# A post-norm attention gate and a top-3 mixture of 12 experts on one core: how the normed rows are split into two f16 parts and transposed, and in which half-turn their transposes, logits and maxima stand

## The reference, cut to what matters

```
o   = sum_k exp(causal scores of the roped q and k)            # one number a row
x1  = layernorm(x + relu(o*fc1_w + fc1_b) @ fc2_w.T + fc2_b)
xa  = x1 @ P_w.T;  C1, C2, C3 = softmax of the 3 largest of 12 logits xa @ U_i.T, else 0
h   = gelu(sum_e C1[:, e] * (x1 @ W1[e].T))
y   = sum_e C2[:, e] * (h @ W2[e].T) + C3 @ b2
out = layernorm(x1 + y)
```

## Time and profile before

| | |
|---|---|
| median of 3 runs | 322.95 us (322.84 to 324.55) |
| profiled execution, its own time | 323.53 us |
| its span, first to last instruction | 321.8 us |
| granted TensorE clock, mean | 0.981 |
| TensorE busy | 282.4 us (88%) |
| VectorE busy | 250.2 us (78%) |
| ScalarE busy | 155.8 us (48%) |
| GpSimd busy | 115.0 us (36%) |
| turns 1 to 5 begin at (C3 transpose) | 139.39, 164.97, 190.55, 216.13, 241.71 us |
| turn 6 and turn 7 begin at | 267.28, 289.77 us |

### The profile page before, as it was taken

One profiled execution on the slowest core, in us unless ns is written; L12 is line 12 of the kernel. 1 busy time (PEld: TensorE's weight loads), 2 busy tenths in 40 slices (PEclk: granted clock), 3 DMA queues, 4 the chain that ended last, 5 costly groups with the idle time before them and its releaser, 6 DMA issues.

```text
span 321.8 us, 6235 instructions
## 1 busy us (share of the span) xinstructions
PE 282.4 (88%) x1976; PEld 191.8 (60%) x1978; DVE 250.2 (78%) x744; ACT 155.8 (48%) x327; POOL 115.0 (36%) x264
## 2 busy tenths in 40 slices
PE   0999999979784989999999999999999997989981
PEld 0444455444333668677677667677678576667770
DVE  0169789999976579689789879888978977887672
ACT  1138747657561381435635634633733753724331
POOL 1000028999999102142332331522333324132221
PEclk9999999999985999999999999999999999999998
DMA  8999999900000000000010001000100010011011
GB/s 232 415 404 229 200 151 211 144 3 0 0 1 0 3 2 0 18 18 18 18 33 17 18 18 29 22 18 18 34 20 16 18 34 19 18 33 26 26 35 37
DMA packets 19235, 20.58 MB, mean 64 GB/s; under 512 B 1600, under 2 KB 18432, under 8 KB 18688
## 3 DMA queue, kind: packets, MB, share of 16 engines
q1 hardware_dynamic: 18480, 19.22, 24.8%
q10 hardware_dynamic: 720, 0.93, 1.0%
HBM read 15.94 MB, written 4.19 MB: 63 GB/s over the span
## 4 chain that ended last, share of the span: by engine, by line
DVE 25%; PE 21%; issue 6%; ACT 5%; POOL 3%; DVEq 0%; POOLq 0%
PE bank L832 17%; DVE early L1202 11%; DVE st L1239 3%; DVE stats L1038 2%; DVE top L1059 2%; ACT x L548 2%; DVE early L1244 2%; PE bank L784 2%; ACT early L657 1%; POOL rstd L391 1%; PE bank L741 1%; DVE mv L1240 1%; ACT x1T L555 1%; ACT early L604 1%; DVE esum L1104 1%
## 5 line engine op out<-in xcount | busy, mean ns | idle before, releaser
L832 PE MATMUL bank<-W,early 128*128 (+1 forms) x630 | 75.5, 273 | 4.4 <-DVE early L1244 2.3
L832 PE MATMUL bank<-W,x1T 128*128 (+1 forms) x630 | 76.9, 277 | 0.5 <-DVE early L1202 0.3
L832 PEld LDWEIGHTS bank<-W,x1T 128*128 128x128 f16 x630 | 60.3, 99 | 19.8 <-DVE early L1202 9.5
L688 PE MATMUL bank<-early,wqk 128*128 128x512 f32 x128 | 64.3, 634 | 8.5 <-DMA gatew<-in_gate 8.5
L1202 DVE SCALAR_TENSOR_TENSOR early<-bank,Csel,early 128x256 f32<-128x256 f32 x124 | 59.3, 479 | 15.0 <-PE bank L832 10.5
L832 PEld LDWEIGHTS bank<-W,early 128*128 128x128 f16 x630 | 60.1, 98 | 14.8 <-DVE early L1244 3.3
L457 POOL TENSOR_SCALAR ve<-mv 128x1 f32<-128x1 f32 x32 | 7.3, 230 | 117.2 <-DVE mv L1240 117.2
L688 PEld LDWEIGHTS bank<-early,wqk 128*128 128x128 f32 x128 | 23.5, 201 | 30.1 <-issue 20.9
L604 ACT ACTIVATE early<-early 128x256 f32<-128x256 f32 x32 | 13.3, 417 | 48.0 <-DVE early L1202 47.9
L499 ACT ACTIVATE qk<-bank 128x512 bf16<-128x512 f32 x32 | 19.0, 594 | 35.6 <-PE bank L688 35.4
L599 ACT ACTIVATE early<-bank,Csel 128x256 f32<-128x256 f32 x31 | 14.6, 472 | 31.0 <-PE bank L832 30.7
(11 more groups left out here) (107 smaller groups left out, 422.3 us busy)
## 6 DMA issues: line engine op xcount, KB each, us to landing
early<-in_xT SPq DMA_DIRECT2D x16, 256.0 KB, 9.8
xs<-in_x SPq DMA_DIRECT2D x32, 128.0 KB, 7.3
out<-early SPq DMA_DIRECT2D x32, 128.0 KB
W<-in_w1T SPq DMA_DIRECT2D x1, 2048.0 KB, 12.0
W<-in_w2T SPq DMA_DIRECT2D x1, 2048.0 KB, 12.3
W<-in_w1T SPq DMA_DIRECT2D x1, 1024.0 KB, 7.6
W<-in_w2T SPq DMA_DIRECT2D x1, 1024.0 KB, 13.8
wqk<-in_wqkT ACTq DMA_DIRECT2D x1, 512.0 KB, 3.8
```

The lines of the kernel that those rows point to most:

```text
L688: mm = pe.matmul(bank[PROJ[n % 2]][:, :], wqk[:, k, g, :], xTb[:, c % 4, k, :, :].rearrange("p s n -> p (s n)"), start=(k == 0), stop=(k = ...
L832: mm = pe.matmul(where[:, 0:DIM], lhs(hx, c), w, start=(k == 0), stop=(k == 5))
```

## The change

For groups 2 to 7 (`ROWWISE = 2`) x1 is split before it is transposed: behind each half of `normed` ScalarE writes the high part of two tiles in row layout into a new tensor xh (128x512, f32 to f16), and GpSimd the low part (x1 minus high part, 128x512). TensorE then transposes eight 128x128 f16 pieces for each half, into the same bank read as f16, and ScalarE copies all 1024 columns of it to x1T in one instruction (`x1T_copy`). VectorE's `x1_low` is gone for these groups. Groups 0 and 1 go the old way. The positions in the turn also change, for all groups of the main stage:

| step | before | after |
|---|---|---|
| TensorE x1_transpose(g, 0), (g, 1) | (2,1), (3,1) | (3,0), next turn's (0,0) |
| TensorE route_logits | (0,1) | (1,0) |
| VectorE route_max | (0,1) | (1,0) |
| VectorE route_strike, two halves | (1,0), (2,0) | both (1,1), behind norm_stats |
| ScalarE exp_route | (1,0) | (2,0), ahead of normed(.., 0) |
| ScalarE bank to x1T, half 0, half 1 | (3,0), (0,0) | (3,1), (0,1) |

```
+        identh = sb("identh", [P, P], F16)
+        xh = sb("xh", [P, 2, 2, 2, DIM], F16)
 (GpSimd)
+            def x1_low(g, h):
+                pool.wait_ge(xhi_done, 2 * (g - ROWWISE) + h + 1)
+                pool.tensor_tensor(xh[:, h, :, 1, :], x1[:, g % 3, 2 * h:2 * h + 2, :], xh[:, h, :, 0, :], ALU.subtract)\
+                    .then_inc(xlo_done, 1)
             def aux(k, s, pos):
-                if (s, pos) == (2, 1) and group(k + 1):
-                    chosen_exps(k + 1)
+                if (s, pos) == (2, 0) and group(k + 2):
+                    x1_low(k + 2, 0)
+                if (s, pos) == (2, 1):
+                    if group(k + 2):
+                        x1_low(k + 2, 1)
+                    if group(k + 1):
+                        chosen_exps(k + 1)
 (ScalarE, end of normed)
+                if g >= ROWWISE:
+                    act.wait_ge(x1_done, 2 * g + h + 1)
+                    if g > ROWWISE:
+                        act.wait_ge(x1T_done, 2 * (g - 1) + h + 1)
+                    act.activation(xh[:, h, :, 0, :], x1[:, g % 3, 2 * h:2 * h + 2, :], ACT.Copy).then_inc(xhi_done, 1)
+            def x1T_copy(g, h):
+                act.wait_ge(x1T_done, 2 * g + h + 1)
+                t = GT * g + 2 * h
+                act.activation(x1T[:, t:t + 2, :, :, :].rearrange("p t l c n -> p (t l c n)"),
+                               bank[XPOSE][:, :].bitcast(F16), ACT.Copy).then_inc(x1lo_done, 1)
             def aux(k, s, pos):
-                if (s, pos) == (1, 0) and group(k + 1):
-                    exp_route(k + 1)
-                if (s, pos) == (2, 0) and group(k + 2):
-                    normed(k + 2, 0)
+                if (s, pos) == (0, 1) and k > 0 and group(k + 1):
+                    x1T_copy(k + 1, 1)
+                if (s, pos) == (2, 0):
+                    if group(k + 1):
+                        exp_route(k + 1)
+                    if group(k + 2):
+                        normed(k + 2, 0)
...
-                if (s, pos) == (3, 0) and group(k + 2):
-                    x1_high(k + 2, 0)
+                if (s, pos) == (3, 1) and group(k + 2):
+                    x1T_copy(k + 2, 0)
 (TensorE, x1_transpose)
+                if g >= ROWWISE:
+                    pe.wait_ge(identh_done, 1)
+                    pe.wait_ge(xlo_done, 2 * (g - ROWWISE) + h + 1)
+                    spread = bank[XPOSE][:, :].bitcast(F16)
+                    for t in range(2):
+                        for l in range(2):
+                            for c in range(NC):
+                                n = 2 * NC * t + NC * l + c
+                                tr = pe.transpose(spread[:, n * P:(n + 1) * P], xh[:, h, t, l, c * P:(c + 1) * P],
+                                                  identh[:, :])
```

More of the change, by code:

```diff
@@ L166, in build @@
         RING, HT = 4, 4
+        ROWWISE = 2
         Z = GT * NR * NE
@@ L202, in build @@
         x1lo_done = sem("x1lo_done")
+        identh_done = sem("identh_done")
+        xhi_done = sem("xhi_done")
+        xlo_done = sem("xlo_done")
         z_done = sem("z_done")
@@ L577, in aux @@
                 if (s, pos) == (0, 0):
-                    if group(k + 1):
-                        x1_high(k + 1, 1)
+                    if k == 0:
+                        x1_high(1, 1)
                     if group(k):
                         C3T_copy(k)
-                if (s, pos) == (1, 0) and group(k + 1):
-                    exp_route(k + 1)
-                if (s, pos) == (2, 0) and group(k + 2):
-                    normed(k + 2, 0)
+                if (s, pos) == (0, 1) and k > 0 and group(k + 1):
[5 more added lines that the diff above has]
+                        normed(k + 2, 0)
                 if (s, pos) == (2, 1) and group(k + 2):
                     normed(k + 2, 1)
-                if (s, pos) == (3, 0) and group(k + 2):
-                    x1_high(k + 2, 0)
+                if (s, pos) == (3, 1) and group(k + 2):
+                    x1T_copy(k + 2, 0)
             def begin(t):
@@ L606, in _ @@
             act.wait_ge(ld_const, 16 * 6)
+            act.activation(identh[:, :], identf[:, :], ACT.Copy).then_inc(identh_done, 1)
             for c in range(NCH):
@@ L738, in x1_transpose @@
                 wait(pe, x1lo_done, 2 * g + h)
+                if g >= ROWWISE:
[8 more added lines that the diff above has]
+                                                  identh[:, :])
+                    tr.then_inc(x1T_done, 1)
+                    return
                 for t in range(2):
@@ L800, in aux @@
             def aux(k, s, pos):
[L801 to L807, removed]
+                if (s, pos) == (0, 0):
+                    if k > 0 and group(k + 1):
+                        x1_transpose(k + 1, 1)
+                    if group(k):
+                        C3_transpose(k)
+                if (s, pos) == (0, 1) and group(k + 2):
+                    fc(k + 2, 1)
+                if (s, pos) == (1, 0) and group(k + 1):
+                    route_logits(k + 1)
                 if (s, pos) == (1, 1) and group(k):
                     bias(k, 0)
-                if (s, pos) == (2, 1):
-                    if group(k):
-                        bias(k, 1)
+                if (s, pos) == (2, 1) and group(k):
+                    bias(k, 1)
+                if (s, pos) == (3, 0):
+                    if group(k + 1):
+                        route_count(k + 1)
                     if group(k + 2):
                         x1_transpose(k + 2, 0)
[L815 to L821, removed]
+                if (s, pos) == (3, 1) and group(k + 3):
+                    fc(k + 3, 0)
             held_ids = {}
@@ L1140, in aux @@
                         fc_add(k + 2, 0)
[L1141 to L1144, removed]
+                    if k == 0:
+                        x1_low(1, 1)
                 if (s, pos) == (1, 0):
@@ L1148, in aux @@
                     if group(k + 1):
-                        route_strike(k + 1, 0)
[L1150 to L1155, removed]
+                        route_max(k + 1)
+                if (s, pos) == (1, 1):
+                    if group(k + 2):
+                        norm_stats(k + 2)
+                    if group(k + 1):
+                        route_strike(k + 1, 0)
                         route_strike(k + 1, 1)
+                if (s, pos) == (2, 0) and group(k):
+                    bias_add(k, 0)
                 if (s, pos) == (2, 1) and group(k + 1):
                     route_mask(k + 1)
[L1159 to L1163, removed]
+                if (s, pos) == (3, 0) and group(k):
+                    bias_add(k, 1)
                 if (s, pos) == (3, 1) and group(k + 1):
```

## The result

| | before | after |
|---|---|---|
| median | 323.13 us (4 runs) | 328.93 us (328.08 to 329.11, 4 runs) |
| ratio | | 1.0165, interval 1.013 to 1.020 |
| profiled execution, span | 323.53, 321.8 us | 329.11, 327.3 us |
| C3 transposes, turns 0 to 7 begin | 101.03, 139.39, 164.97, 190.55, 216.13, 241.71, 267.28, 289.77 | 101.96, 139.53, 166.33, 193.16, 220.00, 246.84, 273.68, 294.98 |

The account below looks back on a forecast made before the run. TensorE (24.19 us busy of a 25.58 us turn) and VectorE (21.95) were taken to bound it, handing work to each other. Turn 0 -1.9, turns 1 to 5 +6.4, turn 6 -0.9: +3.6, 326.6 us, range 321.3 to 330.3.

Parts of the forecast that it names:

- The walk of a full turn: Step-by-step sum of engine queues for turns 1 to 5: 26.87 us against 25.58, +1.29 each, +6.4 for five.
- the second step: Full turn, VectorE overfilled by route_max put in front of norm_stats: transposes at 14.88 against 14.21 before, +0.67 us.
- the third: Full turn, ScalarE's queue with exp and two table loads: gelu to gelu 7.93 us, +1.42 against before.
- the fourth: Full turn, last step: 4.06 us against 4.86, -0.80, as the second x1 transpose and its wait left it.
- the two named losses: Full turns: +0.67 us from VectorE's overfilled second step and +1.42 from ScalarE's queue in the third step.
- TensorE alone would be there at 13.95: Second step: when TensorE by itself would reach the transposes, against 14.88 us by VectorE's path.
- the reserve of 0.27: Third step: TensorE's second mixture ends at 22.54, 0.27 us ahead of the transposes that wait for gelu at 22.81.
- The term of turn 0: Turn 0, with 12 experts in one mixture: turn 1 would begin 1.9 us earlier than at 139.39.
- the adds of the long mixture start 0.8 earlier: Part of the turn 0 gain: VectorE's adds for the 12-expert mixture start 0.8 us earlier.
- The wait of 1.22 us: Turn 0: VectorE's wait for ScalarE's `begin`, which stood behind the table load, was to go.
- Turn 6: Turn with routing but no norm work: forecast 21.57 us instead of 22.49, -0.9.
- The weighed rules: Two skill statements: a 1380 ns drain per table switch, which the trace contradicted, and GpSimd contending with VectorE for SBUF.

Follow-up runs that it names:

- e2_stats_early: Changed kernel with fc_add(k+2, 1) and norm_stats on VectorE moved from (1,0) and (1,1) to (0,1): 322.29 us, ratio 0.994.
- e1_exp_back: Changed kernel with exp_route on ScalarE put back from (2,0) to (1,0): 320.70 us, ratio 0.990.
- e8_mask_early: Changed kernel with route_mask on VectorE at (2,0), ahead of the third step's adds, instead of (2,1): 328.12 us, ratio 1.015.
- e5_positions_alone: Changed kernel with the old split (f32 transposes, x1_low on VectorE) for all groups, new positions kept: 324.01 us, ratio 1.001.
- e7_best: Changed kernel with exp_route at (1,0), route_mask at (2,0), and fc_add and norm_stats at (0,1) except in turn 0: 317.45 us, ratio 0.980.
- e4_split_alone: Changed kernel with every step back at the positions of the kernel before, exp_route at (1,0), row-wise split kept: 334.09 us, ratio 1.032.
- e6_low_twice: Changed kernel with each x1_low on GpSimd done twice, one more subtraction for each half of a group: 332.75 us, ratio 1.026.

## Why the prediction was right

**The walk of a full turn held.** The full turns lose where the prediction said, by +0.7 in the second step, +1.4 in the third, -0.8 in the fourth. Turn 26.87 predicted, 26.84 measured; the second step's transposes at 14.88 behind the C3 transpose, measured 14.92 (208.08 less 193.16); the third step 7.93, measured 7.87; the fourth 4.06, measured 4.04 (215.96 to 220.00). e2_stats_early and e1_exp_back each removed one of the two named losses and left the wait of the other.

**Waits that the walk had otherwise.** It had TensorE wait some 0.9 us for gelu in the second step; it waited 1.19, and for the add ahead of it. "TensorE alone would be there at 13.95" is one pair of transposes too late: the pitches named there sum to 13.58. VectorE's path was last all the same, so this cost the sum nothing. In the third step the walk had no term for the mask. The mask ended behind x1_low (213.28 against 213.04), so TensorE's second mixture ended at 22.80 in place of 22.54 and the reserve of 0.27 was used up: in the trace it ends just where gelu allows the next transposes. That this wait did not set the turn is shown by e8_mask_early.

**Prices.** The xh copy was 0.629 us for 0.63, the subtraction 1.157 for 1.21, eight f16 transposes 0.44 for 0.44, x1T_copy 1.016 for "some 1.0 to 1.2". The 0.63 was a choice between rows of 0.46 and 0.72; that it came out to the digit is luck, and its ends would have moved the turn by 0.2 or 0.3 us.

```profile
L573 ACT ACTIVATE xh<-x x12: 629/629/631, 125.8 to 266.9; 128x512 f16<-128x512 f32 x12
L405 POOL TENSOR_TENSOR xh<-x,xh x12: 1154/1157/1160, 126.5 to 268.0; 128x512 f16<-128x512 f32 x12
```

**What was off by size.** The term of turn 0: "turn 1 begins 1.9 us earlier than at 139.39"; it began 0.14 later. Of the 2 us, 0.93 came ahead of turn 0. Another 0.4 went in its first 13 us, to matmuls at a slower pace. These had a mean clock of 0.86 before and 0.81 here. The rest is the term "the adds of the long mixture start 0.8 earlier": counted from TensorE's transposes of o at the end of that stretch (113.43 before, 114.76 here), they start 9.14 us behind instead of 9.24, 0.1 earlier. The wait of 1.22 us did go, and the two adds that had it start 0.9 us earlier by that measure. But 0.8 of this was lost on VectorE before the long adds: 0.36 from these adds to the low part of hT (with a wait of 0.17 for ScalarE's high part), 0.27 for two strikes that had stood ahead of the wait, and 0.14 at bias_add. What follows the adds came as forecast, 1.09 us shorter for 1.1. Turn 6 was 0.3 us shorter than walked (21.30 for 21.57).

The 0.93 us have this beginning, in the changed kernel:

```profile
8.48 6.74 PE L721 MATMUL bank<-early,wqk 128*128 128x512 f32 x8 [8.48 <-DMA gatew<-in_gate]
15.15 0.63 PE L904 MATMUL bank<-uTs,pws 64*128 64x36 f32 x4
```

From start to start that is 6.67 us; before, the same eight matmuls take 5.64. They run at a pitch of 0.85 us until the clock rises and of 0.43 after, and it rose two to three matmuls later. In the ten experiments, whose beginning is the same as here, the next group starts anywhere from 13.7 to 15.0 us after the span's start (14.17 in the kernel before), and turn 0 at 100.6 to 101.8 (101.03 before, 101.96 here). So nearly all of it is the scatter of one execution and not the change. The profile's +5.5 us holds it; the four executions scatter by 1.7 us in the kernel before and by 1.0 us here.

**The weighed rules.** A table load costs its 1.28 us and the next instruction follows (208.54 to 209.84): the trace again disagrees with the drain that the Trainium skill, "ScalarE: Activation LUTs", section What ACT_TABLE_LOAD costs, adds; with it, by the page's figure and as an estimate, 7.87 would have been 10.6. The other rule showed at a place I had not priced. The mask's first instruction has two SBUF inputs and took 0.55 us beside GpSimd's x1_low in turns 1 to 5, and 0.25 in turns 0 and 6, where GpSimd worked on a 128x1 tile. It took 0.25 in all turns of the kernel before, of e5_positions_alone (same position, no x1_low on GpSimd) and of e7_best (another position). x1_low itself took 1.16 in every instance, beside the mask or not. The trace agrees with the Trainium skill, "GPSIMD Engine Reference", section 8 (Key points), by which VectorE's instructions with two SBUF inputs contend with GpSimd. The timelines of the changed kernel show x1_low, the mask's instruction and, beside the second x1_low, the adds, which read PSUM and stayed as they were (1.00 for the two):

```profile
211.88 1.16 POOL L405 TENSOR_TENSOR xh<-x,xh 128x512 f16<-128x512 f32 x1 [3.86 <-ACT xh L573]
212.60 0.55 DVE L1130 TENSOR_TENSOR mask<-zs,top 128x96 bf16<-128x96 f32 x1
...
214.20 1.00 DVE L1242 SCALAR_TENSOR_TENSOR early<-bank,Csel,early 128x256 f32<-128x256 f32 x2 [0.93 <-ACT early L631]
```

The source views of this instruction, in the changed kernel and in e5_positions_alone:

```profile
L1130 DVE TENSOR_TENSOR mask<-zs,top x7: 248/547/553, 131.4 to 288.3; 128x96 bf16<-128x96 f32 x7
L1125 DVE TENSOR_TENSOR mask<-zs,top x7: 246/248/250, 130.3 to 283.8; 128x96 bf16<-128x96 f32 x7
```

**What stays open.** What each of the small terms in turn 0 is worth was read from timelines only; no run separates them.

## What to carry to other kernels

Where engines hand over in a fixed order every step, a gain of busy time counts only in the step in which that engine is last: sum each engine's queue step by step, not over the turn. An engine at 57% can set the turn by the twelve instructions that stand between two of its hand-overs; side work, and here the table loads above all, belongs into the step in which that engine waits for another. And a named wait is not a cause: moving the mask took a wait of 1.67 us off TensorE and no time off the kernel.

## What the runs showed of the hardware that was not expected

TensorE lost clock after longer waits, and not always. In e4_split_alone it waits 2.30 us at (2,1) in every turn; in four of five the next mixture then ran partly at the lower of the two levels, 1.2 instead of 2.4 GHz. TensorE's timeline of e4_split_alone has one of those turns (18 matmuls in 3.05 us) and the one at full clock (2.13):

```profile
185.00 1.01 PE L779 MATMUL bank<-identh,xh 128*128 128x128 f16 x8 [2.30 <-ACT x L566]
185.81 3.05 PE L876 MATMUL bank<-W,x1T 128*128 x18
...
212.72 0.61 PE L779 MATMUL bank<-identh,xh 128*128 128x128 f16 x8 [2.30 <-ACT x L566]
213.17 2.13 PE L876 MATMUL bank<-W,x1T 128*128 x18
```

Against the turns of the same kernel at full clock such a turn was 1.3 to 1.9 us longer in e4_split_alone and e6_low_twice (one of e4_split_alone, with a clock of 0.88, 2.2), 0.4 to 0.7 in e5_positions_alone, and no longer in the changed kernel, where a wait took it up.

In turns 1 to 5 of the twelve profiles, this stood ahead of the slow stretches: the wait of 2.30 us in four of five turns of e4_split_alone; waits of 1.7 and 0.86 us, 0.25 us of matmuls between them, in three of five of e6_low_twice; and in the changed kernel and e5_positions_alone a wait of 1.19 us in the second step, in one turn of each. That wait, 1.2 to 1.3 us, stands in 25 turns of five kernels, and in 23 of them nothing followed it directly. No slow stretch followed the wait of 1.67 us for the mask in the changed kernel and e2_stats_early (nine turns), nor the one of 1.36 in e8_mask_early (five). The other kernels, without waits over 1.5 us in these turns, had no slow stretch there in their profiles. So the longest waits were followed by it most often, but no bound can be read from these profiles, one execution each. The mean clocks of all executions agree in the main: 0.952 to 0.958 in the four of e4_split_alone, 0.959 to 0.970 in the five of e6_low_twice, 0.971 to 0.981 in the changed kernel. A wait that looks like 1 us in a sum can cost more than that: in e6_low_twice the added wait of 0.86 us made the turn 0.3 to 0.6 us longer at full clock and 2.0 to 2.2 with the slow stretch.
